# Graph attention: the edge projections reach VectorE's addition through PSUM instead of SBUF

## The chip, the cores and the metric

One core of a Trainium2 chip runs the whole program. The metric is device time in microseconds (us). The kernel before was timed three times: median 6233.4 us, from 6230.98 to 6242.8 us. The profile comes from one further execution of 6227.69 us.

## The reference, cut to what matters

Four graph layers run one after the other over 6250 nodes of 128 features and 106250 edges (sorted by their destination). Each is preceded by a layer norm with a ReLU and added to its input. The third, the attention, is the one that matters here:

```python
q = (x @ Wq).reshape(n, H, HD)[src]          # H = 8 heads of HD = 16
k = (x @ Wk).reshape(n, H, HD)[dst]
v_nodes = (x @ Wv).reshape(n, EH, HD)
v = v_nodes[dst]
ek = (edges @ Wek).reshape(-1, H, HD)        # edges: 128 features per edge
ev = (edges @ Wev).reshape(-1, EH, HD)
attn = jnp.einsum('ehd,ehd->eh', q, (k + ek) * scale)
attn = attn @ W_exp
# softmax of attn over the edges of one source node, then
out_e = attn[:, :, None] * (v + ev)
agg = jax.ops.segment_sum(out_e, src, num_segments=n)
out = (v_nodes - agg).reshape(n, EH * HD) @ W_out
```

For every edge the kernel needs k + ek and v + ev: a row of 256 numbers fetched by the destination's number, plus a row of 256 numbers that belongs to the edge.

## The kernel before, in words

The program is a sequence of phases with a full barrier between them. Each phase is a block in which every engine has its own instruction stream, and semaphores order them. An early phase computes the edges' projections (ek and ev side by side, 256 f32 each) and scatters them to DRAM in the order of the source nodes, as the first 256 columns of `by_src0`. A later phase writes the nodes' k and v side by side to the DRAM table `kv`. The phase that the change touches is `attention_edges` (line 1482). It comes after those and before the softmax.

The phase works on tiles of 128 edges, one edge per partition. Eight tiles (G = 8) are a group, there are 112 groups (NG2), and the buffers of a group exist four times (L = 4, index q = g mod 4). For group g:

- SyncE loads the edge projections `ekv` (1024 KB) and a row of source numbers `src_b` spread over the partitions (256 KB), lines 1507 and 1508. Both count on the semaphore `landed[q]`. It stores the sum's v half to DRAM (line 1513) once `kv_ready` shows the additions of g done, and then issues the loads of group g+4 in the same buffers, once the one-hot matrix of g is made.
- GpSimd fetches the node rows: eight indirect DMAs (line 1541), each of 128 rows of 1 KB, into `kv[:, q]`. It waits for the list of indices (`idx_ready`), and from the second round on for the store of v and the products of group g-4.
- ScalarE copies the list of indices of group g+3 (line 1561) as soon as the gathers of g-1 have landed, and in group g evacuates the transposed scores (line 1566) and the logits (line 1572) of group g-1, which it also stores.
- VectorE makes the one-hot matrix of the source numbers of group g+1 (line 1609), waits for the gathered rows of g, adds `ekv` to `kv` in place in two instructions of 128x1024 (line 1620), multiplies the k half by the queries, which stand in PSUM, in two instructions of 128x512 (line 1625), and sums within heads (line 1628).
- TensorE picks the queries of the edges by a product of the one-hot matrix with the queries' table (line 1651, result `p_q` in PSUM), transposes the scores (line 1661) and mixes the heads (line 1668).

The last groups consist of padding: their node numbers are all the same.

Of the kernel before, what the change touches and what calls it, by code (L numbers as in the profile page):

```python
# [24 lines left out]
ALU = mybir.AluOpType  # L25
# [5 lines left out]
P = 128  # L31
N = 6250
E = 106250
D = 128
# [12 lines left out]
NG2 = T2 // G  # L47
# [1434 lines left out]
def attention_edges(nc, K, Dr, s):  # L1482


    L = 4
    C = G // 2
    idx = s.sb("idx", [P, L, G], I32)
    kv, ekv = s.sb("kv", [P, L, G, 2 * D]), s.sb("ekv", [P, L, G, 2 * D])
# [3 lines left out]
    score = s.sb("score", [P, 2, G * H])  # L1492
    scoreT, logit = s.sb("scoreT", [G * H, 2, P]), s.sb("logit", [G * H, 2, P])
    p_q, p_l = s.ps("p_q", [P, 2, 2, C, D]), s.ps("p_l", [G * H, 4, P])
    landed = [s.sem(f"landed{q}") for q in range(L)]
    fetched = K.soft
    prior = [K.soft_count[q] for q in range(L)]
# [3 lines left out]
    idx_ready, shot_ready, q_ready, kv_ready, prod_ready, score_ready, turned, scoreT_ready, mixed, logit_ready, tick = (  # L1501
        s.sem(n) for n in ("idx", "shot", "q", "kv", "prod", "score", "turned", "scoreT", "mixed", "logit", "tick"))
    with nc.Block() as block:
        @block.sync
        def _(sp):
            def load(g, q):
                nc.sync.dma_start(ekv[:, q], Dr.by_src0[bass.ds(g * GE, GE), 0:XM].rearrange("(j p) f -> p j f", p=P)).then_inc(landed[q], 16)
                nc.sync.dma_start(src_b[:, q, :], Dr.rel16[:, bass.ds(g * GE, GE)].broadcast_to([P, GE])).then_inc(landed[q], 16)

            def group(g, q, last):  # L1510
                sp.wait_ge(kv_ready, 2 * g + 2)
                sp.sem_inc(tick, 1)
                nc.sync.dma_start(Dr.v2[bass.ds(g * GE, GE), :].rearrange("(j p) f -> p j f", p=P), kv[:, q, :, D:2 * D]).then_inc(v_stored[q], 16)
                if not last:
                    sp.wait_ge(shot_ready, g + 1)
                    sp.sem_inc(tick, 1)
                    load(g + L, q)

            for q in range(L):
                load(q, q)  # L1520
            with nc.sync.Fori(0, NG2 // L - 1) as i:
                for q in range(L):
                    group(i * L + q, q, False)
            for q in range(L):
                group(NG2 - L + q, q, True)
            for q in range(L):
                sp.wait_ge(v_stored[q], NG2 // L * 16)
# [21 lines left out]
        @block.scalar  # L1549
        def _(act):  # L1550
            act.sem_inc(scoreT_ready, 1)
            act.sem_inc(logit_ready, 1)
            act.sem_inc(l_stored[0], 16)
            act.sem_inc(l_stored[1], 16)

            def numbers(g, q, again):

                if again is not None:
                    act.wait_ge(fetched[q], again * 16 * G + prior[q])
                    act.sem_inc(tick, 1)  # L1560
                nc.scalar.copy(idx[:, q, :], K.srt_dst[:, bass.ds(g * G, G)]).then_inc(idx_ready, 1)

            def scores(g, h):

                act.wait_ge(turned, g + 3)
                nc.scalar.copy(scoreT[:, h, :], p_l[:, 0, :]).then_inc(scoreT_ready, 1)

            def logits(g, h, stores):

                act.wait_ge(mixed, g + 1)  # L1570
                act.wait_ge(l_stored[h], stores * 16 + 16)
                nc.scalar.copy(logit[:, h, :], p_l[:, 1, :]).then_inc(logit_ready, 1)
                act.wait_ge(logit_ready, g + 2)
                act.sem_inc(tick, 1)
                nc.scalar.dma_start(Dr.logit[bass.ds(g * G * H, G * H), :], logit[:, h, :]).then_inc(l_stored[h], 16)

            def group(g, q, stores, again, ahead):

                h = q % 2
                if ahead:  # L1580
                    numbers(g + 3, (q + 3) % L, again)
                if stores is not None:
                    scores(g - 1, 1 - h)
                    logits(g - 1, 1 - h, stores)

            for q in range(3):
                numbers(q, q, None)
            for q in range(L):
                group(q, q, (q - 1) // 2 if q else None, 1 if q else None, True)
            with nc.scalar.Fori(1, NG2 // L - 1) as i:  # L1590
                for q in range(L):
                    group(i * L + q, q, 2 * i + (q + 1) // 2 - 1, i + (q + 3) // L, True)
            for q in range(L):
                group(NG2 - L + q, q, NG2 // 2 - 2 + (q + 1) // 2 - 1, NG2 // L - 1 + (q + 3) // L, q == 0)
            scores(NG2 - 1, 1)
            logits(NG2 - 1, 1, NG2 // 2 - 1)
            for h in range(2):
                act.wait_ge(l_stored[h], NG2 // 2 * 16 + 16)

        @block.vector  # L1600
        def _(dve):
            dve.sem_inc(prod_ready, 4)

            def one_hots(g, q, loads):

                dve.wait_ge(landed[q], loads * 32)
                dve.wait_ge(q_ready, 2 * g)
                dve.sem_inc(tick, 1)
                nc.vector.tensor_scalar(shot[:, q % 2, :], src_b[:, q, :], K.node_col[:, 0:1], None, ALU.is_equal).then_inc(shot_ready, 1)

            def group(g, q, i, last):

                h = q % 2
                if not last:
                    one_hots(g + 1, (q + 1) % L, i + 1 + (q + 1) // L)
                dve.wait_ge(fetched[q], (i + 1) * 16 * G + prior[q])
                dve.sem_inc(tick, 1)
                for c in range(2):
                    both = kv[:, q, C * c:C * c + C, :]
                    nc.vector.tensor_tensor(out=both, in0=both, in1=ekv[:, q, C * c:C * c + C, :], op=ALU.add).then_inc(kv_ready, 1)  # L1620
                for c in range(2):
                    dve.wait_ge(kv_ready, 2 * g + c + 1)
                    dve.wait_ge(q_ready, 2 * g + c + 3)
                    dve.sem_inc(tick, 1)
                    nc.vector.tensor_tensor(out=prod[:, h, C * c:C * c + C, :], in0=p_q[:, h, c], in1=kv[:, q, C * c:C * c + C, 0:D], op=ALU.mult).then_inc(prod_ready, 1)
                dve.wait_ge(prod_ready, 2 * g + 6)
                dve.wait_ge(turned, g + 1)
                nc.vector.tensor_reduce(out=score[:, h, :], in_=prod[:, h].rearrange("p j (h d) -> p (j h) d", d=HD), axis=AX_X, op=ALU.add).then_inc(score_ready, 1)  # L1628

            one_hots(0, 0, 1)  # L1630
            with nc.vector.Fori(0, NG2 // L - 1) as i:
                for q in range(L):
                    group(i * L + q, q, i, False)
            for q in range(L):
                group(NG2 - L + q, q, NG2 // L - 1, q == L - 1)
# [695 lines left out]
def build(nc, A, out):  # L2331
# [13 lines left out]
    with Space(nc, "k") as k:  # L2345
# [43 lines left out]
        with Space(nc, "o") as o:  # L2389
# [19 lines left out]
            with Space(nc, "q") as q:  # L2409
                K.q = q.sb("q", [P, NB + 1, 3, D], BF16)  # L2410
                with Space(nc, "nodes2") as s:
                    nodes_before_attention(nc, K, Dr, s)
                with Space(nc, "edges2") as s:
                    attention_edges(nc, K, Dr, s)
# [53 lines left out]
```

## Time and profile before

| | us |
|---|---|
| median of 3 runs | 6233.4 |
| lowest, highest | 6230.98, 6242.8 |
| the profiled execution, its time | 6227.69 |
| the profiled execution, its span | 6226.5 |
| VectorE busy (61%) | 3776.1 |
| GpSimd busy (60%) | 3731.4 |
| TensorE matmuls busy (58%) | 3638.6 |
| ScalarE busy (23%) | 1425.1 |
| gathers of the attention edges, line 1541, 896 issues | 936.3 |
| additions at line 1620, 224 instructions | 265.1 |

The span runs from the first to the last instruction; the execution's own time is 1.2 us longer. The busy times are sums over the whole span, and the phases differ much from each other. The attention edges run from about 3172 to 4420 us after the span's start. An indirect DMA on GpSimd is shown for as long as GpSimd works at issuing it; the transfer comes after.

### The profile page before, as it was taken

The numbers are of one execution on the slowest core, as the hardware profiler recorded it, in microseconds if no ns is written. First come the engines' busy times: TensorE is split into PE (matmuls) and PEld (weight loads), VectorE is DVE, ScalarE is ACT, GpSimd is POOL, SyncE is SP. The second block draws the span as 40 slices with busy tenths as digits, with TensorE's granted clock in tenths as the row PEclk, the third lists the DMA queues.
The fourth block names the chain that finished last, engine by engine and source line by source line (L and its number), as shares of the span: only waits on it lengthen the run. The fifth ranks groups of instructions, "written<-read, shape, count | busy, mean of one in ns | idle before, by whom it ended". The sixth has DMA issues, their size and how long they took to land. (4 is left out here: it accounts for less than half of the span.)

```text
span 6226.5 us, 102739 instructions
## 1 busy us (share of the span) xinstructions
PE 3638.6 (58%) x22653; PEld 2924.5 (47%) x22654; DVE 3776.1 (61%) x8537; ACT 1425.1 (23%) x3681; POOL 3731.4 (60%) x3791
## 2 busy tenths in 40 slices
PE   7768888888795333333444444444056655567756
PEld 5546666666573333333432222222045545566655
DVE  9858888888796333434554444444578854444444
ACT  7635555555003000000110000000023321111112
POOL 0057777777111777777447777777134427777774
PEclk9969999999896555555665555555579966655567
DMA  3069889998441121212168888888554422222221
GB/s 106 4 195 283 283 285 286 285 286 257 96 102 45 53 52 52 52 52 52 34 217 270 268 268 272 265 271 250 88 140 135 136 71 58 58 58 58 58 58 54
DMA packets 906276, 920.78 MB, mean 148 GB/s; under 512 B 329944, under 2 KB 744746, under 8 KB 906090
## 3 DMA queue, kind: packets, MB, share of 16 engines
q1 hardware_dynamic: 755002, 542.66, 31.2%
q0 software_dynamic: 138544, 371.96, 18.8%
q10 hardware_dynamic: 12672, 5.51, 0.4%
q8 instruction: 21, 0.34, 0.0%
q14 instruction: 37, 0.30, 0.0%
HBM read 678.28 MB, written 241.47 MB: 148 GB/s over the span
## 5 line engine op out<-in xcount | busy, mean ns | idle before, releaser
L1541 POOL DMA_INDIRECT edges_kv<-kv,edges_idx x896 | 936.3, 1045 | 428.7 <-issue 269.0
L961 POOL DMA_INDIRECT by_src<-edges_rows,edges_pos x832 | 891.3, 1071 | 255.3 <-issue 247.1
L2112 POOL DMA_INDIRECT sum_rows<-table,sum_idx x832 | 806.5, 969 | 343.7 <-issue 253.2
L1272 POOL DMA_INDIRECT sum_rows<-table,sum_idx x832 | 788.2, 947 | 363.6 <-issue 251.7
L1349 PE MATMUL sum_p_sum<-sum_hot,sum_rows 128*128 128x128 f32 x1664 | 387.4, 427 | 663.9 <-DMA sum_rows<-table,sum_idx 663.9
L1349 PEld LDWEIGHTS sum_p_sum<-sum_hot,sum_rows 128*128 128x128 f32 x1664 | 359.9, 328 | 691.5 <-issue 691.5
L1620 DVE TENSOR_TENSOR edges_kv<-edges_kv,edges_ekv 128x1024 f32<-128x1024 f32 x224 | 265.1, 1224 | 625.8 <-DMA edges_kv<-kv,edges_idx 625.8
L2211 PE MATMUL sum_p_sum<-sum_hot,sum_msg 128*128 128x128 f32 x1664 | 382.4, 423 | 402.2 <-DVE a_acc L2171 396.6
L1328 DVE TENSOR_TENSOR a_acc<-a_acc,sum_p_sum 128x128 f32 x832 | 235.1, 283 | 550.2 <-PE sum_p_sum L1349 549.2
L2211 PEld LDWEIGHTS sum_p_sum<-sum_hot,sum_msg 128*128 128x128 f32 x1664 | 358.1, 327 | 423.4 <-issue 423.4
L733 PE MATMUL edges_p_attr<-k_wekv,edges_attr 128*128 128x256 f32 x1664 | 473.7, 434 | 134.2 <-ACT edges_rows L808 127.8
L1651 PE MATMUL edges_p_q<-q_q,edges_src_hotT 128*128 x2688 | 380.5, 286 | 134.3 <-issue 86.1
L1818 POOL TENSOR_TENSOR sum_wv<-sum_vv,sum_wv 128x1024 f32<-128x1024 f32 x112 | 217.7, 1944 | 388.9 <-ACT sum_wv L1827 388.9
L2156 DVE TENSOR_TENSOR sum_msg<-sum_p_msg,sum_rows 128x512 f32<-128x512 f32 x208 | 134.0, 686 | 496.2 <-DMA sum_rows<-table,sum_idx 496.2
L733 PEld LDWEIGHTS edges_p_attr<-k_wekv,edges_attr 128*128 128x128 f32 x1664 | 339.6, 215 | 188.3 <-ACT edges_rows L808 135.7
L1651 PEld LDWEIGHTS edges_p_q<-q_q,edges_src_hotT 128*128 128x128 bf16 x2688 | 279.8, 104 | 258.7 <-issue 198.8
L1911 PE MATMUL sum_p_sum<-sum_wv,sum_hot 128*128 128x136 f32 x1792 | 300.5, 320 | 142.6 <-DVE sum_hot L1862 114.4
L1661 PE MATMUL edges_p_l<-k_ident,edges_score 128*64 128x128 f32 x112 | 44.2, 394 | 571.7 <-DVE edges_score L1628 571.7
L1311 DVE TENSOR_SCALAR sum_hot<-k_lane,k_dst_f,k_ew 128x128 f32<-128x128 f32 x832 | 300.8, 363 | 89.6 <-issue 89.1
L1911 PEld LDWEIGHTS sum_p_sum<-sum_wv,sum_hot 128*128 128x128 f32 x1792 | 257.6, 216 | 176.9 <-issue 176.9
L808 ACT COPY edges_rows<-edges_p_attr 128x512 f32<-128x512 f32 x416 | 224.0, 586 | 498.8 <-DMA by_src<-edges_rows,edges_pos 473.3
L2171 DVE TENSOR_TENSOR a_acc<-a_acc,sum_p_sum 128x128 f32 x832 | 239.5, 288 | 96.5 <-DVE a_acc L2171 0.8
(375 smaller groups left out, 7724.1 us busy)
## 6 DMA issues: line engine op xcount, KB each, us to landing
edges_ekv<-by_src SPq DMA_DIRECT2D x112, 1024.0 KB
v<-edges_kv SPq DMA_DIRECT2D x112, 512.0 KB, 4.0
sum_vv<-v SPq DMA_DIRECT2D x112, 512.0 KB, 3.9
edges_attr<-in_attr128T SPq DMA_DIRECT2D x104, 512.0 KB
edges_near<-h_in SPq DMA_DIRECT2D x832, 48.0 KB
sum_rows<-by_src SPq DMA_DIRECT2D x112, 264.0 KB, 3.0
edges_src_b<-rel SPq DMA_DIRECT2D x112, 256.0 KB
edges_dst_b<-dst SPq DMA_DIRECT2D x104, 256.0 KB
```

Of the source, the lines that this page charges most:

```text
L733: mm = nc.tensor.matmul(p_attr[:, c % 2, j, :], attr[:, q, (2 * c + j) * P:(2 * c + j + 1) * P], K.wekv[:], start=True, stop=True)
L961: nc.gpsimd.indirect_dma_start(Dr.by_src0, bass.IndirectOffsetOnAxis(pos[:, q, j:j + 1], 0), rows[:, q % 2, j, :], None).then_inc(scattere ...
L1272: nc.gpsimd.indirect_dma_start(rows[:, q, j, :], None, Dr.table, bass.IndirectOffsetOnAxis(idx[:, q, j:j + 1], 0)).then_inc(fetched[q], 16)
L1311: ins = nc.vector.tensor_scalar(hot[:, h, j, :], K.lane[:, 0:P], to, weight, ALU.is_equal, ALU.mult)
L1349: mm = nc.tensor.matmul(p_sum[:, c, j % 4, :], rows[:, q, j, :], hot[:, h, j, :], start=True, stop=True)
L1541: nc.gpsimd.indirect_dma_start(kv[:, q, j, :], None, Dr.kv, bass.IndirectOffsetOnAxis(idx[:, q, j:j + 1], 0)).then_inc(fetched[q], 16)
L1620: nc.vector.tensor_tensor(out=both, in0=both, in1=ekv[:, q, C * c:C * c + C, :], op=ALU.add).then_inc(kv_ready, 1)
L1651: mm = nc.tensor.matmul(p_q[:, h, c, j % C, :], shot[:, h, j * P:(j + 1) * P], K.q[:, bass.ds(blk[j], 1), k, :].rearrange("p a d -> p (a d)"),
L1911: mm = nc.tensor.matmul(p_sum[:, c, bass.ds(slot[j], 1), 0:W].rearrange("p a f -> p (a f)"), hot[:, h, j, :], wv[:, h, j, :], start=False, ...
L2112: nc.gpsimd.indirect_dma_start(rows[:, q, j, :], None, Dr.table, bass.IndirectOffsetOnAxis(idx[:, q, j:j + 1], 0)).then_inc(fetched[q], 16)
L2171: nc.vector.tensor_tensor(out=place, in0=place, in1=p_sum[h][:, j // 4, j % 4, :], op=ALU.add).then_inc(added, 1)
L2211: mm = nc.tensor.matmul(p_sum[h][:, c, j % 4, :], msg[:, h, j, :], hot[:, h, j, :], start=True, stop=True)
```

## The change

A PSUM tile `p_e` of two buffers holds two tiles' projections each (128x512 f32). ScalarE copies the loaded projections into it, two tiles at a time, four copies per group (`pair`). VectorE adds them to the gathered rows from there, in four instructions of 128x512 instead of two of 128x1024. A copy into a buffer waits for the addition that last read it. ScalarE makes the first two copies of group g+1 at the end of its group g, once `landed` of g+1 has come; the first two copies of group 0 stand ahead of everything else that ScalarE does, the first lists of indices included. `kv_ready` now counts four per group.

```diff
+    p_e = s.ps("p_e", [P, 2, 2, 2 * D])
+    e_ready = s.sem("e")
...
             def group(g, q, last):
-                sp.wait_ge(kv_ready, 2 * g + 2)
+                sp.wait_ge(kv_ready, 4 * g + 4)
...
+            def pair(q, c):
+
+                nc.scalar.copy(p_e[:, c % 2], ekv[:, q, 2 * c:2 * c + 2, :]).then_inc(e_ready, 1)
+
+            def group(g, q, stores, again, ahead, loads):
...
                 if stores is not None:
                     scores(g - 1, 1 - h)
                     logits(g - 1, 1 - h, stores)
+                for c in (2, 3):
+                    act.wait_ge(kv_ready, 4 * g + c - 1)
+                    pair(q, c)
+                if loads is not None:
+                    act.wait_ge(landed[(q + 1) % L], loads * 32)
+                    act.sem_inc(tick, 1)
+                    for c in (0, 1):
+                        act.wait_ge(kv_ready, 4 * g + c + 3)
+                        pair((q + 1) % L, c)
+
+            act.wait_ge(landed[0], 32)
+            for c in (0, 1):
+                pair(0, c)
 
             for q in range(3):
                 numbers(q, q, None)
...
                 dve.wait_ge(fetched[q], (i + 1) * 16 * G + prior[q])
                 dve.sem_inc(tick, 1)
+                for c in range(4):
+                    both = kv[:, q, 2 * c:2 * c + 2, :]
+                    dve.wait_ge(e_ready, 4 * g + c + 1)
+                    nc.vector.tensor_tensor(out=both, in0=both, in1=p_e[:, c % 2], op=ALU.add).then_inc(kv_ready, 1)
                 for c in range(2):
-                    both = kv[:, q, C * c:C * c + C, :]
-                    nc.vector.tensor_tensor(out=both, in0=both, in1=ekv[:, q, C * c:C * c + C, :], op=ALU.add).then_inc(kv_ready, 1)
-                for c in range(2):
-                    dve.wait_ge(kv_ready, 2 * g + c + 1)
+                    dve.wait_ge(kv_ready, 4 * g + 2 * c + 2)
                     dve.wait_ge(q_ready, 2 * g + c + 3)
```

The other changed lines pass the count of loads to ScalarE's `group`.

## Rows read from the trace of the kernel before

**Rows 1.** The page, section 2: GpSimd's busy tenths in 40 slices.
```profile
POOL 0057777777111777777447777777134427777774
```

**Rows 2.** The waits of 3170 to 4425 us: who waited for whom, us, times, longest.
```profile
DVE edges_kv L1620 <- DMA edges_kv<-kv,edges_idx: 625.8, 110, 10.8
...
POOL edges_kv L1541 <- ACT edges_idx L1561: 135.4, 10, 132.6
...
POOL edges_kv L1541 <- DMA v<-edges_kv: 24.1, 2, 23.8
```

**Rows 3.** Two lines' instructions (ns minimum/median/maximum), then the group of 3200 to 4300 us.
```profile
L1541 POOL DMA_INDIRECT edges_kv<-kv,edges_idx x896: 940/946/2002, 3172.4 to 4403.8; - x180
...
L1272 POOL DMA_INDIRECT sum_rows<-table,sum_idx x832: 940/944/1042, 1998.3 to 3038.8; - x167
...
L1541 POOL DMA_INDIRECT edges_kv<-kv,edges_idx x814 | 852.6, 1047 | 247.9 <-issue 245.5 <-ACT edges_idx L1561 2.4
```

**Rows 4.** The timeline, GpSimd: start us, us, line, names, idle before and its releaser.
```profile
3172.37 0.94 POOL L1541 DMA_INDIRECT edges_kv<-kv,edges_idx  x1 [132.61 <-ACT edges_idx L1561]
...
3187.37 1.60 POOL L1541 DMA_INDIRECT edges_kv<-kv,edges_idx  x1 [0.30 <-ACT edges_idx L1561]
...
4314.16 1.47 POOL L1541 DMA_INDIRECT edges_kv<-kv,edges_idx  x1 [0.30 <-issue]
...
4317.18 0.94 POOL L1541 DMA_INDIRECT edges_kv<-kv,edges_idx  x1 [0.30 <-issue]
```

**Rows 5.** The timeline of 3403 to 3421 us, VectorE, GpSimd and SyncE's queue.
```profile
3403.57 2.37 DVE L1620 TENSOR_TENSOR edges_kv<-edges_kv,edges_ekv 128x1024 f32<-128x1024 f32 x2 [5.80 <-DMA edges_kv<-kv,edges_idx]
...
3404.79 1.96 POOL L1541 DMA_INDIRECT edges_kv<-kv,edges_idx  x1 [0.30 <-issue]
...
3406.19 0.40 SPq L1513 DMA_DIRECT2D v<-edges_kv  x1
...
3407.06 0.95 POOL L1541 DMA_INDIRECT edges_kv<-kv,edges_idx  x1 [0.30 <-issue]
...
3419.46 0.48 DVE L1609 TENSOR_SCALAR edges_src_hotT<-edges_src_b,k_node_col 128x1024 bf16<-128x1024 bf16 x1
3419.58 1.18 POOL L1541 DMA_INDIRECT edges_kv<-kv,edges_idx  x1 [0.30 <-issue]
```

**Rows 6.** One line's instructions, then groups by line (busy us, mean ns, idle).
```profile
L1328 DVE TENSOR_TENSOR a_acc<-a_acc,sum_p_sum x832: 271/282/291, 2012.1 to 3048.3; 128x128 f32 x167
...
L1625 DVE TENSOR_TENSOR edges_prod<-edges_p_q,edges_kv 128x512 f32<-128x512 f32 x204 | 130.6, 681 | 0.0
L1628 DVE TENSOR_REDUCE edges_score<-edges_prod 128x64 f32<-128x1024 f32 x102 | 124.4, 1220 | 3.5
...
L1831 ACT COPY sum_p_sum<-sum_none 128x544 f32<-128x544 f32 x224 | 138.1, 617 | 319.5 <-DVE den_sums L1878 311.4 <-DVE sum_none L1854 8.1
...
L1566 ACT COPY edges_scoreT<-edges_p_l 64x128 f32<-64x128 f32 x112 | 28.9, 258 | 614.7 <-PE edges_p_l L1661 614.7
```

**Rows 7.** The page's DMA issues (us to landing), and the first gather of group 24.
```profile
v<-edges_kv SPq DMA_DIRECT2D x112, 512.0 KB, 4.0
...
3429.82 1.18 POOL L1541 DMA_INDIRECT edges_kv<-kv,edges_idx  x1 [0.30 <-issue]
```

**Rows 8.** The timeline of the phase's start, ScalarE and VectorE.
```profile
3171.37 0.49 ACT L1561 COPY edges_idx<-o_srt_dst 128x8 int32<-128x8 int32 x4 [4.13 <-PEq L1405]
...
3179.51 0.48 DVE L1609 TENSOR_SCALAR edges_src_hotT<-edges_src_b,k_node_col 128x1024 bf16<-128x1024 bf16 x1 [8.70 <-DMA edges_src_b<-rel]
```

**Rows 9.** Windows: us, busy (x) of PE, PEld, DVE, ACT, POOL, PE clock, DMA share, GB/s.
```profile
3170.00:3200.00 30.00, 11.28 (x75) 7.91 (x75) 9.49 (x13) 1.41 (x8) 21.24 (x22) 0.50 0.95 312
3200.00:3250.00 50.00, 21.31 (x130) 13.98 (x130) 23.20 (x28) 3.37 (x14) 38.52 (x38) 0.50 0.90 283
3250.00:4200.00 950.00, 387.87 (x2356) 253.99 (x2355) 455.42 (x528) 62.28 (x262) 736.38 (x702) 0.51 0.86 269
4330.00:4370.00 40.00, 11.12 (x67) 7.06 (x65) 15.12 (x17) 1.69 (x7) 30.86 (x31) 0.50 0.92 124
```

More of the change, by code:

```diff
@@ L1575, in logits @@
                 nc.scalar.dma_start(Dr.logit[bass.ds(g * G * H, G * H), :], logit[:, h, :]).then_inc(l_stored[h], 16)
-            def group(g, q, stores, again, ahead):
+            def pair(q, c):
+                nc.scalar.copy(p_e[:, c % 2], ekv[:, q, 2 * c:2 * c + 2, :]).then_inc(e_ready, 1)
+            def group(g, q, stores, again, ahead, loads):
                 h = q % 2
@@ L1588, in _ @@
             for q in range(L):
-                group(q, q, (q - 1) // 2 if q else None, 1 if q else None, True)
+                group(q, q, (q - 1) // 2 if q else None, 1 if q else None, True, 1 + (q + 1) // L)
             with nc.scalar.Fori(1, NG2 // L - 1) as i:
                 for q in range(L):
-                    group(i * L + q, q, 2 * i + (q + 1) // 2 - 1, i + (q + 3) // L, True)
+                    group(i * L + q, q, 2 * i + (q + 1) // 2 - 1, i + (q + 3) // L, True, i + 1 + (q + 1) // L)
             for q in range(L):
-                group(NG2 - L + q, q, NG2 // 2 - 2 + (q + 1) // 2 - 1, NG2 // L - 1 + (q + 3) // L, q == 0)
+                group(NG2 - L + q, q, NG2 // 2 - 2 + (q + 1) // 2 - 1, NG2 // L - 1 + (q + 3) // L, q == 0, NG2 // L if q < L - 1 else None)
             scores(NG2 - 1, 1)
```

## The prediction

> **What bounds the kernel now.** The page comes first. The change touches one phase, the attention edges, which runs from 3172 to 4420 us, about a fifth of the span. The line of slices shows GpSimd busy at seven or eight tenths all through it [rows 1]. The waits inside the phase come next [rows 2]. VectorE sits idle 625.8 us before its first addition, waiting for the gathered rows. GpSimd, which issues those gathers, waits for another engine only at both ends: 132.6 us of its 135.4 us is the time before the phase begins, and 24.1 us falls near the end. In between it issues one gather after another. So GpSimd's issuing sets the pace, and the question is what makes one issue long.
>
> The durations answer it [rows 3]. The median of an issue is 946 ns, the longest is 2002 ns, and the mean over the steady part is 1047 ns. The phase that gathers for the graph convolution has issues of the same kind with a median of 944 ns and a maximum of 1042 ns. There 832 issues start from 1998.3 to 3038.8 us, so one starts every 1040.5/831 = 1.252 us and eight take 10.02 us. In our phase group 0 starts at 3172.37 and group 106 at 4317.18, which is 10.80 us per group [rows 4]. The missing 0.78 us per group, 83 us over 106 groups, is stall; 814 x (1047 - 946) ns = 82 us says the same from another view [rows 3].
>
> The timeline shows what stalls them [rows 5]. An issue at 3404.79 takes 1.96 us. It began while the second of two additions at line 1620 was running (3403.57 to 3405.94), and was done about 0.8 us after that addition ended. The next issue, at 3407.06 beside the product and the reduction of lines 1625 and 1628, took 0.95 us. The issue at 3419.58, which began 0.12 us into the one-hot instruction of line 1609, took 1.18 us. I laid every issue of groups 0 to 105 beside the VectorE instructions that it overlaps. 100 of them were lengthened beside line 1620 by 64.9 us in total (the first at 3187.37, the last at 4314.16), and 86 beside line 1609 by 19.1 us (the one at 3419.58 is typical); those beside lines 1625 and 1628 alone kept 946 ns. Sum 84.0 us, so the stall is accounted for [rows 4, 5].
>
> **The change part by part.** *The additions.* Two additions of 128x1024 with both inputs in SBUF go; four of 128x512 come, with the gathered rows in SBUF and the projections in PSUM. The graph convolution's own addition has exactly this order, first input in SBUF and second in PSUM, and runs 832 times beside gather issues that keep 944 ns [rows 3, 6]. The product at line 1625, with the PSUM input first, leaves them alone as well. I therefore let the whole 64.9 us go. The other end is 0, if what counts is the addition itself; the rows are near the first end.
>
> The Trainium skill speaks against this. Its page "SBUF — State Buffer", section "Who interferes with whom", says that a VectorE instruction with two SBUF inputs meets GpSimd only where GpSimd reads, and infers that `tensor_tensor` does not hold up descriptor generation, since that needs the write interface. By it nothing would be won here. The trace disagrees with the inference: the 1.96 us beside line 1620 against the 0.95 us of its neighbours [rows 5].
>
> *The one-hot of line 1609.* It stays, but now it stands at a fixed distance behind the additions whose end released GpSimd, and so it meets the start of an issue again and again, at 0.12 us. With nothing to lock the two, an issue must start within 0.36 us or so of a 1.25 us cycle to be held, and the wait is 0.23 us or less: from 0 (never met) to 112 x 0.3 = 34 us (always met at the worst place). Chance meetings would leave some 4 us, today's pattern 19; I take 7, a gain of 12.
>
> *The copies on ScalarE.* Four of 128x512 f32 from SBUF into PSUM. ScalarE has such a copy at 128x544: 617 ns [rows 6], so 0.59 us each, 2.4 us per group. ScalarE's own work there is three copies of at most 0.26 us [rows 6] in 10.8 us, so it has room. The order matters more: the list of indices for group g+3 now stands behind the copies of g-1 and g, and these behind the additions of g-1. It comes some 3.6 us after the rows of g-1 have landed. GpSimd needs it, with the store of v, much later: for group 20 the additions start at 3403.57, the store of v is issued at 3406.19 and lands 4.0 us on, at 3410.2, and GpSimd begins group 24 at 3429.82 [rows 5, 7]. 19.6 us of slack cover the later indices and the later store, so I cost them at nothing; with the cover gone each would cost its own 0.4 to 3.6 us per group.
>
> *VectorE's own time.* Additions with PSUM run at the rate of line 1625 (681 ns for 512 columns), 4 x 0.68 = 2.7 us against the 2.37 us that two of today's take [rows 5, 6]. Copy and addition alternate over two buffers: copies 0 and 1 are made ahead, copy 2 waits for addition 0. Addition 0 ends at 0.68, copy 2 at 0.68 + 0.04 + 0.59 = 1.31, just before addition 1 ends at 1.36, so there is hardly a gap: about 2.8 us in all, +0.4 us. VectorE's group is then 2.8 + 1.36 (two products) + 1.22 + 0.48 = 5.9 us of 10.1: hidden. It costs once, 0.4 us, at the last group. The store of v and the next load go out 0.4 us later, with the same 19.6 us of cover.
>
> *The start.* ScalarE now waits for the first projections and their index row before it makes any list of indices. Before, the lists were made at 3171.37 and GpSimd began at 3172.37. The one-hot that waits for the same landings ran at 3179.51 [rows 8]. Add two copies, 1.2 us, and the step of 0.8 us from the end of the first list to the first issue: 3181.7, or 9 us late. Without the gathers beside them the loads may land a little sooner; bounds 4 to 10, I take 8. GpSimd is the pace from here to the tail, so all of it counts.
>
> *The tail.* From 4330 us the transfer engines are 92% busy at 124 GB/s against 269 before [rows 9]: the last groups are slow by their transfers, and GpSimd waits 24.1 us for the store of v [rows 2]. That stretch moves as a block and keeps its length; nothing is won in it.
>
> Sum: -64.9 - 12 + 8 + 0.4 = -68 us. The profiled execution took 6227.7 us (span 6226.5), 5.7 below the median of the runs shown, 6233.4. So 6159 for a like execution, and 6165 for the median.
>
> **The rivals.** *A. The transfers become the pace.* A group now moves 269 GB/s x 10.80 us = 2.91 MB at a busy share of 0.86. At 10.1 us per group that is 288 GB/s at 0.92. For it: 50 us of the phase's start show 283 GB/s at 0.90 with GpSimd never waiting. Against it: its first 30 us show 312 GB/s at 0.95 [rows 9]. If 0.90 is all that holds over a millisecond, a group takes 0.86 x 10.80/0.90 = 10.3 us, the gain is 106 x 0.48 = 51 less 8, and the time 6190.
>
> *B. The stall isn't the second SBUF input.* Then the additions stall GpSimd as before, only the late start stays: 6233 + 8 = 6241. For it: no 128x512 addition in the new order was seen beside a gather issue. Against it: the 832 of 128x128 that were [rows 3, 6]. The Trainium skill's inference (the page "SBUF — State Buffer", the section named above) would lead to the same end.
>
> *C. The handshake becomes the pace, and the kernel is slower.* Place: the alternation of copies and additions. It decides once VectorE's group passes 10.8 us: 10.8 - 3.1 = 7.7 us for four additions, 1.9 us each. With the copies wholly in the open a pair takes 0.59 + 0.68 + 0.1 = 1.4 us, 5.5 us in all, a group 8.6 us, still hidden. A copy into PSUM would have to take over 1.1 us and not overlap. At 2 us a copy, a group takes 14 us: +3.4 x 112 = 380 us, 6610. The 617 ns row speaks against it.
>
> *D. GpSimd's phase against line 1609 locks at its worst.* 34 us stay instead of 7: 6192.
>
> **How the numbers follow.** Forecast 66% (with its own range 6146 to 6183), A 14%, D 6%, B 9%, C 5%. The lower end, 6144, has no stall left at all and the small start, 6233 - 84 + 4, less some scatter of the runs; the upper, 6203, takes in A and D with the start of 10 us and scatter. B and C lie outside. Within 0.2% of before, 12 us, is what a measurement can't tell from no change: B falls there almost whole, 9%, with a small part of the rest. Faster 86%, same 9%, slower 5%.
>
> **What would show each step.** The gather issues at a mean of 950 to 965 ns, none over 1.3 us beside an addition; groups 0 to 106 at 10.1 us each; the wait of VectorE for the gathered rows shorter per group, by about 1 us; copies at 0.59 us and additions at 0.68 us; the first gather issue 8 us later after the phase begins; the tail with its 24 us wait as it was; in the steady part 285 to 290 GB/s. A mean issue near 1040 ns would refute the main step and speak for B. Issues at 950 ns with GpSimd waiting for the store of v in the middle of the phase would speak for A; VectorE's waits for ScalarE of over 2 us per group for C; issues of 1.18 us and longer beside line 1609 in nearly every group for D.

## The result and the profile after

The changed kernel takes 6170.58 us (median of 4 runs, 6167.57 to 6172.21) against 6233.88 us before (4 runs, 6230.98 to 6242.8): ratio 0.9896, 95% interval 0.9878 to 0.9913, 63.3 us less. The forecast was 6165. Its profile has a span of 6166.3 us, 60.2 less than the span before.

GpSimd's issues come first, as in [rows 3]: the line's durations (ns minimum/median/maximum), then its group from 3200 to 4200 us (count, busy us, mean ns, idle us and its cause), then two issues of the timeline, the first of group 0 and the first of group 106.

```profile
L1543 POOL DMA_INDIRECT edges_kv<-kv,edges_idx x896: 942/946/1208, 3186.5 to 4338.9; - x180
...
L1543 POOL DMA_INDIRECT edges_kv<-kv,edges_idx x797 | 757.9, 951 | 242.8 <-issue 242.8
...
3186.50 0.94 POOL L1543 DMA_INDIRECT edges_kv<-kv,edges_idx  x1 [141.33 <-ACT edges_idx L1563]
...
4251.10 0.95 POOL L1543 DMA_INDIRECT edges_kv<-kv,edges_idx  x1 [0.30 <-issue]
```

The mean fell from 1047 to 951 ns and the longest from 2002 to 1208 ns. A group takes (4251.10 - 3186.50)/106 = 10.04 us instead of 10.80. The timeline of one group shows why.

```profile
3401.20 2.63 DVE L1640 TENSOR_TENSOR edges_kv<-edges_kv,edges_p_e 128x512 f32<-128x512 f32 x4 [1.82 <-DMA edges_kv<-kv,edges_idx]
...
3401.31 0.94 POOL L1543 DMA_INDIRECT edges_kv<-kv,edges_idx  x1 [0.30 <-issue]
3401.92 1.19 ACT L1581 COPY edges_p_e<-edges_ekv 128x512 f32<-128x512 f32 x2 [0.91 <-DVE edges_kv L1640]
3402.55 0.94 POOL L1543 DMA_INDIRECT edges_kv<-kv,edges_idx  x1 [0.30 <-issue]
...
3406.20 0.48 DVE L1628 TENSOR_SCALAR edges_src_hotT<-edges_src_b,k_node_col 128x1024 bf16<-128x1024 bf16 x1
3406.30 1.19 POOL L1543 DMA_INDIRECT edges_kv<-kv,edges_idx  x1 [0.30 <-issue]
```

Two issues begin while additions run (3401.31 and 3402.55), and both take 0.94 us, where one that began in an addition of the kernel before took 1.96 us [rows 5]. In groups 0 to 105 there are 223 such issues, and none of them is lengthened by more than 20 ns. The one-hot instruction, which reads SBUF alone, still holds the issue that begins 0.10 us into it: 1.19 us. The waits of 3170 to 4370 us (who waited for whom, us, times, longest) and the windows answer to [rows 2, 9].

```profile
DVE edges_kv L1640 <- DMA edges_kv<-kv,edges_idx: 509.1, 102, 10.4
ACT edges_p_e L1581 <- DVE edges_kv L1640: 469.4, 214, 21.7
...
POOL edges_kv L1543 <- DMA v<-edges_kv: 28.0, 2, 16.6
DVE edges_kv L1640 <- ACT edges_p_e L1581: 17.4, 10, 1.9
```
```profile
3250.00:4200.00 950.00, 420.69 (x2558) 275.64 (x2557) 511.17 (x759) 285.81 (x663) 719.39 (x758) 0.50 0.92 290
...
4270.00:4310.00 40.00, 9.91 (x57) 6.24 (x57) 14.03 (x21) 7.78 (x19) 20.78 (x22) 0.50 0.94 111
```

VectorE waited for a copy 17.4 us in the whole phase, and for the gathered rows 509.1 us where it was 625.8 [rows 2]; the transfers carry 290 GB/s at 0.92 instead of 269 at 0.86; the tail is the slow stretch that it was. The start is the cost that the change brings. The first row is from before, the others from after.

```profile
3171.59 0.38 SPq L1507 DMA_DIRECT2D edges_ekv<-by_src  x1
```
```profile
3177.45 0.38 SPq L1509 DMA_DIRECT2D edges_ekv<-by_src  x1
...
3184.47 1.11 ACT L1581 COPY edges_p_e<-edges_ekv 128x512 f32<-128x512 f32 x2 [11.82 <-DMA edges_src_b<-rel]
...
3185.51 0.49 ACT L1563 COPY edges_idx<-o_srt_dst 128x8 int32<-128x8 int32 x4
```

From the first load's issue to the first gather issue it was 0.78 us [rows 8], and is 3186.50 - 3177.45 = 9.05 us.

The difference of the two spans, by stretch:

| stretch | before | after | difference |
|---|---|---|---|
| span's start to the phase's first load | 3171.6 | 3177.5 | +5.9 |
| first load to first gather issue | 0.8 | 9.1 | +8.3 |
| first gather of group 0 to that of group 106 | 1144.8 | 1064.6 | -80.2 |
| from there to the last v store's landing | 101.8 | 103.6 | +1.8 |
| from there to the end | 1807.5 | 1811.6 | +4.1 |

The sum is -60.1 us. Only the three middle rows hold changed code, -70.1 us in all. Of the 80.2 us, 64.8 is stall beside the additions (64.9 before, 0.15 in 5 issues now) and 14.8 stall beside the one-hot instruction (19.1 in 86 issues before, 4.3 in 38 now). The first and last rows, +10.0 us, hold none. The code ahead of the phase is the same in four kernels that took 6159 to 6236 us, and their traces have the phase's first load at 3171.6 (before), 3177.5 (after), 3177.5 (Idle instructions, below) and 3185.6 us (Wide copies, below), so +5.9 us is no more than its scatter.

One thing must be known for the numbers below: in three of the four sets of experiments every kernel ran over 1000 us slower than at first (7259, 7358 and 7263 us for the kernel before, against 6234), though one of these sets used the same chip as the fourth, where all was as at first.

### The profile page after: what moved, and what is told of

Read it like the earlier page. It is cut to its first block and busy times, and to the rows that moved or that the text cites. A ratio compares the mean times of both kernels' runs of the same rounds, so it can differ in the third digit from the quotient of the medians.

```text
span 6166.3 us, 104207 instructions
## 1 busy us (share of the span) xinstructions
PE 3666.2 (59%) x22653; PEld 2949.4 (48%) x22654; DVE 3798.5 (62%) x8761; ACT 1685.0 (27%) x4129; POOL 3651.1 (59%) x3791
## 3 DMA queue, kind: packets, MB, share of 16 engines
q0 software_dynamic: 138544, 371.96, 19.1%
## 5 line engine op out<-in xcount | busy, mean ns | idle before, releaser
L1543 POOL DMA_INDIRECT edges_kv<-kv,edges_idx x896 | 851.8, 951 | 443.0 <-issue 273.6
L1640 DVE TENSOR_TENSOR edges_kv<-edges_kv,edges_p_e 128x512 f32<-128x512 f32 x448 | 287.9, 684 | 532.6 <-DMA edges_kv<-kv,edges_idx 509.1
L1328 DVE TENSOR_TENSOR a_acc<-a_acc,sum_p_sum 128x128 f32 x832 | 235.3, 283 | 549.1 <-PE sum_p_sum L1349 548.0
L1581 ACT COPY edges_p_e<-edges_ekv 128x512 f32<-128x512 f32 x448 | 263.3, 589 | 490.0 <-DVE edges_kv L1640 469.4
L1931 PE MATMUL sum_p_sum<-sum_wv,sum_hot 128*128 128x136 f32 x1792 | 320.2, 335 | 126.7 <-DVE sum_hot L1882 99.3
L1931 PEld LDWEIGHTS sum_p_sum<-sum_wv,sum_hot 128*128 128x128 f32 x1792 | 275.9, 230 | 160.7 <-issue 160.7
```

The costliest lines, as they stand in the source:

```text
L1543: nc.gpsimd.indirect_dma_start(kv[:, q, j, :], None, Dr.kv, bass.IndirectOffsetOnAxis(idx[:, q, j:j + 1], 0)).then_inc(fetched[q], 16)
L1581: nc.scalar.copy(p_e[:, c % 2], ekv[:, q, 2 * c:2 * c + 2, :]).then_inc(e_ready, 1)
L1640: nc.vector.tensor_tensor(out=both, in0=both, in1=p_e[:, c % 2], op=ALU.add).then_inc(kv_ready, 1)
L1931: mm = nc.tensor.matmul(p_sum[:, c, bass.ds(slot[j], 1), 0:W].rearrange("p a f -> p (a f)"), hot[:, h, j, :], wv[:, h, j, :], start=False, ...
```

## The experiments

Twelve runs were made in four sets. The three slow sets are called hindered here, and the other condition the first. Times in them are set against the kernel before of the same set. The median length of a gather issue is the same in both conditions (946 to 949 ns, kernel before and changed kernel), and so the issues are read apart from the time. What the expectations call slower chips is this condition.

**The base once more (hindered set).** The changed kernel, unedited.

> The changed kernel once more, unedited, as the base of this set. Every theory: 6170 us (6166 to 6174), groups 0 to 106 at 10.04 us each, a mean gather issue of 951 ns, and the first gather issue about 9 us after the phase's first load is issued. What differs from its first profile before and behind the phase is the scatter of one execution against the next.

Measured: 7409.56 us against 7259.24, ratio 1.0192 (1.0173 to 1.0211), 13.72 us per group; the mean issue was 951.6 ns, as expected. The time was not. Here the change costs 1.9%, though its issues are as short as ever. The windows of 3800 to 5100 us, kernel before (of the next experiment) and changed kernel, in this condition:

```profile
3800.00:5100.00 1300.00, 462.13 (x2682) 288.91 (x2682) 522.96 (x599) 71.39 (x299) 823.67 (x807) 0.50 0.72 225
```
```profile
3800.00:5100.00 1300.00, 435.17 (x2510) 270.10 (x2509) 492.44 (x744) 273.81 (x650) 710.52 (x748) 0.51 0.69 208
```

The transfer engines are less busy than in the first runs (0.72 and 0.69 against 0.86 and 0.92), so it isn't transfers that hold here. VectorE's waits of the changed kernel (3770 to 5220 us) name ScalarE's copies and no longer the gathers, and GpSimd now waits for the store of v, which stands behind the late additions:

```profile
DVE edges_kv L1640 <- ACT edges_p_e L1581: 603.4, 74, 23.2
DVE edges_kv L1640 <- issue: 282.9, 28, 18.2
DVE edges_kv L1640 <- DMA edges_kv<-kv,edges_idx: 14.2, 2, 9.8
...
POOL edges_kv L1543 <- DMA v<-edges_kv: 257.2, 36, 16.3
```

**The kernel before, profiled in this condition.**

> The kernel before, unedited, for a profile from the same chip as the others of this set. In the set before, every kernel ran slower in all phases (the kernel before 7259 us, its changed form 7410), with transfers of 210 GB/s where 285 were moved at first. If this chip does as the first one, every theory: 6234 us, 10.80 us per group, gather issues of 1045 ns. If it does as the second: 7260 us; theory T (there the transfers are the pace and GpSimd waits for the store of v) 12.5 to 13 us per group with GpSimd waiting in most groups; rival (GpSimd still the pace) no such waits.

Measured: 7352.61 us, 12.79 us per group, issues of 1020 ns with 61.0 us of stall beside the additions, so GpSimd still loses there what it lost at first, but it also waits 232 us at the starts of groups. Theory T was wrong: the waits name the store of v in no group, and the transfers were 0.72 busy. Nor was GpSimd still the pace, as the rival had it. VectorE's waits (3770 to 5120 us) show that the rows were nearly always there when VectorE came for them:

```profile
DVE edges_prod L1625 <- remote: 629.7, 56, 25.9
DVE edges_prod L1625 <- PE edges_p_q L1651: 95.1, 67, 17.4
...
DVE edges_kv L1620 <- DMA edges_kv<-kv,edges_idx: 10.9, 3, 5.2
```

It waited 10.9 us for rows, where it was 625.8 at first [rows 2], and over 700 us in front of the products. ("remote" is a release whose instruction the profile doesn't name. Line 1625 waits only for VectorE's own additions and for the queries, so it is the queries.) The pace here lies with TensorE and what it waits for, not with GpSimd's issues. The timeline of TensorE shows another thing, matmuls of line 1651 that start 1.4 us apart where twelve of them usually take 1.5 us:

```profile
4406.67 0.27 PE L1651 MATMUL edges_p_q<-q_q,edges_src_hotT 128*128 x1 [1.23 <-issue]
4408.20 0.26 PE L1651 MATMUL edges_p_q<-q_q,edges_src_hotT 128*128 x1 [1.26 <-issue]
4409.62 0.27 PE L1651 MATMUL edges_p_q<-q_q,edges_src_hotT 128*128 x1 [1.16 <-issue]
```

**Lists of indices first.** Run in two hindered sets.

```diff
+            for q in range(3):
+                numbers(q, q, None)
             act.wait_ge(landed[0], 32)
             for c in (0, 1):
                 pair(0, c)
-            for q in range(3):
-                numbers(q, q, None)
```

> ScalarE makes the first three lists of indices before it waits for the first projections. Theory (GpSimd's issuing is the pace from its first issue on, so its late start is paid in full): first gather issue 0.8 us after the first load's issue instead of 9.05, the same 10.04 us per group, so 8 us less, 6162 us. Rival (the late start costs nothing, since the first rows and loads would land no sooner, or the tail takes it back): 6170 us.

> Lists of indices ahead of the wait for the first projections, again. Where gather issues are the pace (the kernel before at 6234 us): first issue 0.8 us after the first load's issue, 10.04 us per group, 6162 us; rival (start costs nothing) 6170. Where the transfers are the pace: as the changed kernel within 0.3%, 1.02 of the kernel before.

Measured: 7394.19 us, ratio 1.0192 (1.0171 to 1.0213), and 7527.3 us, ratio 1.0216 (1.0181 to 1.0252). From the first load to the first gather issue it was 0.78 us in both. That the late start can be taken away is shown; what it saves these sets can't tell (8 us are 0.1%). The last kernel below has the same edit.

**Additions from SBUF, copies and waits kept.** Also in two hindered sets.

```diff
-                    nc.vector.tensor_tensor(out=both, in0=both, in1=p_e[:, c % 2], op=ALU.add).then_inc(kv_ready, 1)
+                    nc.vector.tensor_tensor(out=both, in0=both, in1=ekv[:, q, 2 * c:2 * c + 2, :], op=ALU.add).then_inc(kv_ready, 1)
```

> ScalarE's copies and all waits stay as changed, but VectorE's four additions of 128x512 read the projections from SBUF, not from PSUM. Theory (the second SBUF input holds an issue that starts within the addition until it ends): issues lengthened beside the additions again, each by less than before, since an addition now ends after 0.68 us: about two issues per group held 0.17 us each, 0.36 us per group or 38 us over 106 groups, 10.4 us per group, 6208 us (6195 to 6225). Rival (the narrower instructions with pauses between them free GpSimd, not the place of the input): 10.04 us per group, 6170 us.

> The four additions read the projections from SBUF, copies and waits as changed, again. Where gather issues are the pace: theory (second SBUF input holds GpSimd) 10.4 us per group, 6208 us (6195 to 6225), mean issue about 990 ns, as the 992 ns of the set before; rival (narrower instructions free GpSimd) 10.04 us per group and 6170 us. Where the transfers are the pace the issues are held all the same and the time says nothing of it.

Measured: 7427.88 us, ratio 1.0232 (1.0205 to 1.0259), and 7565.72, ratio 1.0254 (1.0213 to 1.0295). What it tells stands in the issues. The first row is this kernel from 3850 to 5200 us, the second the changed kernel of the same set:

```profile
L1543 POOL DMA_INDIRECT edges_kv<-kv,edges_idx x757 | 752.3, 994 | 599.2 <-issue 355.1 <-DMA v<-edges_kv 243.8 <-ACT edges_idx L1563 0.3
```
```profile
L1543 POOL DMA_INDIRECT edges_kv<-kv,edges_idx x781 | 743.2, 952 | 607.3 <-issue 371.1 <-DMA v<-edges_kv 236.2
```

With the projections in SBUF the issues are held again, 38.5 us in 111 issues over 106 groups (38.0 in the second set), where 38 was expected. Of 140 issues that begin in an addition, 108 are lengthened. With the projections in PSUM (the changed kernel of the same set) 137 issues begin in an addition and none is lengthened; some 5 us of stall remain there, in about 30 issues that begin in the one-hot instruction. The same four instructions with the same waits differ in the place of one input alone. The time of the first condition, 6208 us by the theory, was not tried.

**Reads only.** Four more additions per group, both inputs SBUF, the result into PSUM.

```diff
+                dve.wait_ge(kv_ready, 4 * g + 4)
+                for c in range(4):
+                    dve.wait_ge(x_done, 4 * g + c + 1)
+                    nc.vector.tensor_tensor(out=p_x[:], in0=kv[:, q, 2 * c:2 * c + 2, :], in1=kv[:, q, 6 - 2 * c:8 - 2 * c, :], op=ALU.add).then_inc(x_done, 1)
```

> The changed kernel with four more VectorE additions of 128x512 per group, both inputs the gathered rows in SBUF, the result into a spare PSUM bank that nothing reads. VectorE writes nothing to SBUF in them. VectorE's group becomes 5.9 + 2.9 = 8.8 us, still under 10. Theory R (the second SBUF read is what holds a gather issue): issues lengthened beside the new line, about 0.36 us per group, mean issue near 990 ns; where issues are the pace 10.4 us per group, 6208 us. Rival W (the issue is held by VectorE's writes to SBUF, the reads are free, as an inference of the Trainium skill has it): issues stay at 951 ns, 6170 us.

Measured: 7690.07 us, ratio 1.0436 (1.0390 to 1.0481), in a hindered set; mean issue 979 ns. Its timeline:

```profile
4428.35 2.90 DVE L1646 TENSOR_TENSOR edges_p_x<-edges_kv 128x512 f32<-128x512 f32 x4
4429.27 1.32 POOL L1544 DMA_INDIRECT edges_kv<-kv,edges_idx  x1 [0.30 <-issue]
4430.89 1.16 POOL L1544 DMA_INDIRECT edges_kv<-kv,edges_idx  x1 [0.30 <-issue]
```

105 issues were lengthened beside the new line, by 25.6 us. VectorE writes nothing to SBUF there, so no write to SBUF is needed for the hold, and the second SBUF read is enough: theory R. Its size was less than the 38 us expected, and the time, taken in a hindered set, says nothing of it. The Trainium skill (page "SBUF — State Buffer", "Who interferes with whom") infers that `tensor_tensor` leaves descriptor generation alone. For the issue of an indirect DMA the runs contradict it: 1.32 us beside this line, against 0.94 us alone. They fit the page's other sentence, that a VectorE instruction with two SBUF inputs contends with a GpSimd instruction that reads SBUF, since the second input comes through the shared read interface; which interface it is no run shows.

**One buffer.** One PSUM buffer, each copy behind the addition before it.

```diff
-    p_e = s.ps("p_e", [P, 2, 2, 2 * D])
+    p_e = s.ps("p_e", [P, 1, 2, 2 * D])
...
-                for c in (2, 3):
-                    act.wait_ge(kv_ready, 4 * g + c - 1)
+                for c in (1, 2, 3):
+                    act.wait_ge(kv_ready, 4 * g + c)
...
```

> One PSUM buffer for the projections instead of two: each of copies 1 to 3 waits for the addition before it, so copies and additions alternate in the open, (0.59 + 0.68 + 0.1) x 3 + 0.68 = 4.8 us per group instead of 2.8. Theory (VectorE and ScalarE are off the path, GpSimd's issuing is the pace): 10.04 us per group, mean issue 951 to 955 ns, 6170 to 6173 us. Rival (the handshake is near the path): 2 us per group more show, up to 6370 us.

Measured: 7446.79 us against 7259.24, ratio 1.0263 (1.0245 to 1.028), 0.7 points over the changed kernel. The issues stayed short (947 ns). In this condition VectorE isn't off the path, and that the longer handshake shows for this reason is likely but not read from a trace: the profiled execution was the fastest of six (7398.4 us) and had 13.48 us per group, less than the 13.72 of the changed kernel. The run says nothing of the first condition, for which it was meant.

**The added wait alone.** The kernel before with one wait more.

```diff
                 for c in range(2):
+                    if c == 1:
+                        dve.wait_ge(logit_ready, g + 1)
                     both = kv[:, q, C * c:C * c + C, :]
```

> The kernel before, with one wait more: the second addition of group g waits until ScalarE has made the logits of group g-1. No copies, no PSUM, nothing else changed: the dependency of the changed kernel alone. Theory H: on a slower chip the ratio to the kernel before is 1.02 to 1.04 (the changed kernel's loss, without its shorter gather issues), the two additions take 8 to 11 us as a block instead of 2.4. Rival K (the copies as such, not the order behind the logits): 0.998 to 1.005. On a chip that behaves as the first one both expect 10.80 us per group and 6234 us.

Measured: 7336.58 us against 7262.53, ratio 1.009 (1.007 to 1.0111), 13.31 us per group, the two additions 10.3 us as a block. VectorE's waits (3750 to 5150 us):

```profile
DVE edges_kv L1622 <- ACT edges_logit L1572: 633.9, 80, 29.7
DVE edges_kv L1622 <- issue: 212.9, 24, 20.4
```

The wait costs 0.9%, neither the 2 to 4% of theory H nor the nothing of rival K. The changed kernel has this dependency by the order of ScalarE's work: copies 2 and 3 of group g stand behind the logits of g-1, which wait for TensorE.

**Copies ahead of the logits.**

```diff
+                for c in (2, 3):
+                    act.wait_ge(kv_ready, 4 * g + c - 1)
+                    pair(q, c)
                 if stores is not None:
                     scores(g - 1, 1 - h)
                     logits(g - 1, 1 - h, stores)
-                for c in (2, 3):
...
```

> The changed kernel with ScalarE's copies 2 and 3 of a group moved ahead of its two copies for the scores and logits of the group before. Theory H (on the slower chips the change loses because additions 2 and 3 of group g stand behind ScalarE's logits of g-1, which wait for TensorE's queries, transposition and mixing): there the block of four additions falls from 10.8 us towards 3 to 5 us, the group from 13.7 to 12.3 to 12.9 us, the ratio to the kernel before from 1.019 to 0.995 to 1.005. Rival K (ScalarE itself pauses there, in whatever order it has its work, and the additions now depend on it at all): the block stays over 8 us and the ratio at 1.015 to 1.025. On a chip that behaves as the first one both expect 10.04 us per group and 6170 us, since VectorE waited for a copy only 17 us in all.

Measured: 7386.76 us against 7262.53, ratio 1.0172 (1.0151 to 1.0192). VectorE's waits (3750 to 5180 us):

```profile
DVE edges_prod L1645 <- remote: 781.3, 81, 25.2
DVE edges_kv L1640 <- ACT edges_p_e L1581: 41.5, 50, 3.1
```

The block of additions did fall, from 10.8 to 2.6 us, as theory H had it, and the group stayed at 13.66 us: VectorE now waits almost as long in front of the products, for TensorE's queries. So the wait moved, the time stayed, and neither theory accounts for the loss.

**Idle instructions.** The kernel before with more ScalarE instructions and no more work.

```diff
+                for _ in range(13):
+                    act.sem_inc(tick, 1)
```

> The kernel before with 13 more instructions per group on ScalarE that do nothing but add one to a semaphore that nobody waits for, while ScalarE is idle. No data, no dependency, no PSUM. On the slower chips a group took 87 ns for each instruction that the trace holds of it, in the kernel before (12.8 us, 147 instructions) and in the changed one (13.7 us, 159). Theory N (there the number of instructions issued, whatever they do, sets the pace): 159 instructions, 13.7 us per group, ratio 1.012 to 1.020. Theory H/K (the additions' dependency on ScalarE's copies costs it): the ticks are free, 12.8 us per group, ratio 0.998 to 1.003. On a chip that behaves as the first one both expect 6234 us.

Measured: 6236.27 us against 6233.75, ratio 1.0001 (0.9991 to 1.0012). This set ran in the first condition, where both expected it, so theory N was not tried.

**Wide copies, ahead, lists first.** Two copies and two additions of 128x1024 through one buffer of two banks. The lines are set against the changed kernel; the edit of "Lists of indices first" is in it as well.

```diff
-    p_e = s.ps("p_e", [P, 2, 2, 2 * D])
+    p_e = s.ps("p_e", [P, C, 2 * D])
...
+                act.wait_ge(kv_ready, 2 * g + 1)
+                pair(q, 1)
                 if stores is not None:
...
-                for c in range(4):
-                    both = kv[:, q, 2 * c:2 * c + 2, :]
+                for c in range(2):
+                    both = kv[:, q, C * c:C * c + C, :]
...
```

> Projections through PSUM in two copies of 128x1024 into one buffer of two banks, two additions of 128x1024 from there, the second copy ahead of the scores' copies, the lists of indices ahead of everything at the start. Copy 1 waits for addition 0, so the block is 1.22 + 1.0 + 1.22 + 0.1 = 3.5 us. About 152 instructions per group. On a slower chip theory N: 13.2 us per group, ratio 1.003 to 1.009; theory H/K (ScalarE in the additions' chain, however many instructions): as e7, 13.7 us, ratio 1.014 to 1.020. On a chip that behaves as the first one both: no issue held by an addition, 10.0 us per group, first issue 8 us sooner than in the changed kernel, 6160 to 6164 us.

Measured: 6158.87 us against 6233.75 in its set, ratio 0.9876 (0.9861 to 0.9891), the shortest time of all. The line's durations, and its timeline:

```profile
L1543 POOL DMA_INDIRECT edges_kv<-kv,edges_idx x896: 940/946/1191, 3186.4 to 4334.8; - x180
```
```profile
3401.78 1.22 DVE L1637 TENSOR_TENSOR edges_kv<-edges_kv,edges_p_e 128x1024 f32<-128x1024 f32 x1 [5.87 <-DMA edges_kv<-kv,edges_idx]
3402.02 0.94 POOL L1543 DMA_INDIRECT edges_kv<-kv,edges_idx  x1 [0.30 <-issue]
3403.04 1.02 ACT L1581 COPY edges_p_e<-edges_ekv 128x1024 f32<-128x1024 f32 x1 [7.71 <-DVE edges_kv L1637]
```

This is the cleanest answer to whether narrower instructions free GpSimd. The additions are as wide and as long as before the change (1.22 us), and the issue that begins 0.24 us into one takes 0.94 us. Of 208 issues that begin in one of these additions none is lengthened by more than 20 ns. The group took 10.03 us although copy 1 lies in the open (block of additions 3.5 us, VectorE waits 121 us for copies in the phase): that is hidden. The first gather issue came 0.77 us after the first load, 8.3 us sooner than in the changed kernel, and the medians differ by 11.7 us, or their ratios by 0.2 points with intervals that overlap: in line with the start, not proof of it.

## Why the prediction was right

- *What sets the pace.* Right in the first condition. GpSimd issued without a wait from group 0 to 109, before and after, and the time fell with the issues. It was luck that the result was taken in this condition: in the hindered one GpSimd isn't the pace, and the forecast has no term for it.
- *The additions, -64.9 us.* Right: 0.15 us stay. That the place of the second input does it, not the width or the pauses, is shown by the additions from SBUF (38.5 us of stall come back, same width and same waits) and by the wide ones from PSUM (none).
- *The one-hot, -12.* Measured -14.8, with the reason given: the issues lengthened beside it fell from 86 to 38. Before, an issue began within 0.24 us of the start of the one-hot in 104 of the first 106 groups; after, the starts spread over the whole 1.25 us of an issue's cycle. The 7 us that were to stay lay between a chance meeting (4 us) and the old pattern (19); 4.3 stayed.
- *The start, +8.* Measured +8.3.
- *The copies and VectorE's time, nothing.* Right: copies 589 ns (0.59), additions 684 ns (0.68), the block 2.8 us (2.8), slack in front of GpSimd's next round 18 us.
- *Rival A.* 0.92 busy at 290 GB/s held for a millisecond, so 0.90 was no ceiling. *B* fell with the first row. *D* didn't come.
- *Rival C, slower by a handshake,* was priced by the length of a copy, and didn't come in the first condition. In the hindered sets the changed kernel was slower, but not by this mechanism: the copies took 588 ns, as always, and what came late was ScalarE's turn for them. The prediction had listed what the indices wait for behind the copies, and not what the copies wait for behind the logits. Even that is not the whole cause, since the loss stayed at 1.7% when VectorE hardly waited for copies any more (41.5 us).
- The forecast was 68 us, 63.3 were measured. The changed stretches gave 70.1; the rest lies in phases that the change doesn't touch. The runs of the kernel before lie 12 us apart.

What stays open: why everything ran slower in three sets (the transfers were less busy, and in this phase TensorE's matmuls came late and one by one), and why the changed kernel loses 1.9% there. The coupling of the additions to ScalarE's logits costs 0.9% by itself; the rest is unexplained, and with the copies moved ahead the ratio is 0.2 points lower, with intervals that overlap. That the number of instructions sets the pace there was expected of one run and could not be tried. A first run alone would not have shown that the gain hangs on the condition.

## What to carry to other kernels

Where GpSimd issues indirect DMAs one after another, look at the longest issue, not at the median. If it is twice as long and began in a VectorE addition with two SBUF inputs, the addition held it here, and with one of these inputs in PSUM it did not. What that is worth hangs on what sets the pace: 1.0% was won where GpSimd did, and 1.9% lost where VectorE waited for TensorE. Where a copy is put in front of such an instruction, read the whole queue of the engine that makes it: what its copies stand behind is now in VectorE's path. And keep what starts the slowest engine (here the first lists of indices) ahead of new waits.

## What the runs showed of the hardware that was not expected

- The hold has a sharp form. In the kernel before, an issue that begins in an addition is lengthened by what is left of the addition (1.22 us) less about 0.13 us: one that begins 0.05 us in by 1.04 us, one 1.0 us in by 0.10. One that begins within 0.03 us of the addition's start, or before it, is not held, and VectorE waited little (1.21 to 1.30 us for every addition).
- The same chip ran the kernel before in 7259 us in one set and in 6234 us in another, and the changed kernel, in the slower of these sets 7410 us against 6171, kept its lengths: gather issues 946 ns in the median in both traces, copies 589 and 588 ns, additions 684 and 681.
- ScalarE writes PSUM from SBUF at the pace at which it reads it: 128x1024 in 1016 ns, where the copy of the k and v rows out of PSUM took 1012.
